# A recommendation tower on one core: the order of a few VectorE steps, look-ups and one load in the first tile's batches 0 to 2

## The chip, the cores and the metric

The kernel runs on one core of a Trainium2 chip. The metric is the device time of one execution in microseconds (us). The engines are named as in the profile: PE (TensorE) multiplies matrices, with its weight loads as PEld; DVE (VectorE), ACT (ScalarE) and POOL (GpSimd) are the others; SP and ACT also issue direct DMAs, POOL the gathers. Each engine works through its own list of instructions in order and waits at semaphores for the others.

## The reference, cut to what matters

```python
e = jnp.stack([tbl_0[ids[:, 0]], ..., tbl_38[ids[:, 38]]], axis=1)      # 2048 x 39 x 32
p = inputs[:, ROW, :]                # the 741 pairs i < j of the 39 fields
q = inputs[:, COL, :]
z = jnp.einsum('bpc,apc,bpa->bp', p, w, q)       # w: 32 x 741 x 32
h = jnp.concatenate([z, dense_ctx], axis=1)
h = jnp.maximum(h @ W_top1 + b_top1, 0.0)        # 757 -> 512
h = jnp.maximum(h @ W_top2 + b_top2, 0.0)        # 512 -> 256
y = h @ W_top3
```

Thirty-nine embedding tables are looked up, every pair of fields gives one number through its own 32x32 matrix, and three layers follow. The tables have 1,000 to 125,000 rows.

## The kernel before, in words

The 2048 rows are cut into 4 tiles of 512 (`NT`, `NB`). The 39 fields are cut into 10 chunks of up to four (`NG`, `C`); a chunk of a tile is written (t, g). The pairs are grouped into 200 units (`UNITS`): a unit is the product of one field j of chunk g with the four fields of chunk gi, so one 128-row matmul. Two units make a step, two steps a batch, and a tile has 50 batches (`NBAT`).

A batch b is, on PE: two steps of `interact` (L590, u_ps <- e4, w4: pair weights times the field stacked four times), then `reduce` of batch b-1 (L614, z_ps: sums over 32 rows), then what tables of numbers put there. A step waits until the products of two steps before are made. On DVE: `multiply` (L911), two products of 128x1024, prod <- u_ps, eT; then splits, one-hots and weights as the tables say.

A chunk comes in by one or both of two ways into one accumulator, `t_ps`. Fields in large tables are gathered by POOL (L419, `indirect_dma_start`), and turned on PE (`turn`, L534). Fields in small tables ("hot", `HOT_TABLES`: chunks 1, 2, 7, 8) are looked up: for each slice k, DVE makes a one-hot in bf16 (`one_hot_slice`, L899) and PE multiplies it by three bf16 parts of the table (`look_up`, L553). A slice holds up to four fields. Chunk 7 has ten slices: slices 0 to 7 have four fields (12 matmuls; on DVE one instruction of 125x1536 with `row8` and one of 125x512 with `row10`), slices 8 and 9 one field (3 matmuls, one instruction of 125x512). There are three one-hot buffers (`OS`): DVE waits at slice n for the look-up of slice n-3.

When `t_ps` is full, ACT takes it (`take_chunk`): parts <- t_ps (L717), the high part, and eT <- t_ps (L722). Only then may the next chunk use `t_ps`. DVE makes the low part (`split_chunk`, L865: eT minus the high part). In the first tile, chunks 1, 0, 2, 3, 7 (`MADE`) are stacked without memory: PE repeats the parts (`make_half`, L571, two fields of the chunk at a time, into m_ps and z_ps) and ACT copies them to e4 (`take_half`, L734 and L735). The second half waits for the copy of the first. All other chunks are stored by SP to memory (`scratch`) and come back stacked.

`FIRST_TILE` says for each chunk of tile 0 in which batch it is turned and in which batch each slice is looked up; from it come `TAKES` (batch to slices), `COMPLETE` (batch in which a chunk is complete) and the rest. DVE makes a batch's one-hots one batch ahead: after the products of batch b, it makes the slices of `TAKES[b+1]`. Chunk 2 is complete in batch 1; its first use is the second step of batch 2 (unit 10). Chunk 3 is first used in batch 5, chunk 7 in batch 9.

The pair weights are split too, in 13 pieces of 16 units (`PREP_UNITS`): ACT loads a piece (`load_weights`, L741), rounds it to the high part (L748) and stores that to `w_rows` (L751), DVE makes the low part (`weights_low`, L872), ACT stores it (L758). `PREPS` says in which batch a piece is made ({1: 2, 3: 3, 6: 4, ...}), `PREP_LOADS` in which it is loaded ({2: 3, 4: 4, 6: 5, ...}). Two rooms alternate, so piece 3's load waits only for piece 1's stores. SP brings finished pieces to PE as w4 (L436).

POOL's first 96 gathers are not paced by the products: gather n waits for the landing of gather n-3. In tile 0 the gathers 0 to 15 are chunk 0's, 16 to 19 chunk 2's, 20 to 35 chunk 3's, 36 to 51 chunk 4's, 52 to 67 chunk 5's. The turn of chunk 4 stands on PE in batch 7, after that batch's `reduce`. SP issues the five loads of the MLP's weights (L504) in batch 7.

Of the kernel before, what the change touches and what calls it, by code (L numbers as in the profile page):

```python
# [21 lines left out]
def fields_in(g):  # L22
    return min(C, F - C * g)
# [23 lines left out]
def slice_fields(g, k):  # L47

    return [x for x, n in enumerate(HOT_SLICES[g]) if n > k]
# [41 lines left out]
def place_sums():  # L91
# [4 lines left out]
    for g, gi, j in UNITS:  # L96
# [9 lines left out]
        if room > n:  # L106
# [24 lines left out]
PREP_UNITS = [(16 * k, min(NU, 16 * k + 16)) for k in range(-(-NU // 16))]  # L131
PREPS_FIRST = 2
PREPS = {max(4 * k - 11, 2 * k - 3 if k < 4 else 6): k for k in range(PREPS_FIRST, len(PREP_UNITS))}

PREP_LOADS = {max(2 if k == 3 else 4, 4 * k - 15, k + 1 if k > 4 else 0): k for k in range(3, len(PREP_UNITS))}

BEGIN = (1, 0)
FIRST_TILE = ((2, 0, 0, (0, 0, 0, 1, 1, 1, 1, 1)), (7, 0, None, (1, 1, 1, 1, 1, 2, 2, 2, 2, 2)), (3, 0, 3, ()), (4, 0, 7, ()),  # L140
# [9 lines left out]
MADE = ((0, 1), (0, 0), (0, 2), (0, 3), (0, 7))  # L150
# [8 lines left out]
def chunks_of_tile(t):  # L159
    return [x for x in (OTHER_TILES if t else FIRST_TILE) if t + x[1] < NT]  # L160

# [54 lines left out]
for t in range(NT):  # L216
    for g, nxt, turn, slices in chunks_of_tile(t):
        c = (t + nxt, g)
# [62 lines left out]
def tower(nc, tables, ids, hot_ids, hot_rows, dense, w, w1, b1, w2, b2, w3, sel_in, ident_in, y):  # L281
# [4 lines left out]
    with ExitStack() as ctx:  # L286
# [106 lines left out]
        def e_slot(t, g):  # L393
            return NG + TWO_PLACES.index(g) if t % 2 and g in TWO_PLACES else g
# [308 lines left out]
        def _(act):  # L703
# [33 lines left out]
            def load_weights(k):  # L737
                a, b = PREP_UNITS[k]
                if k >= 2:
                    act.wait_ge(s_wout[k % 2], 64 * (k // 2))  # L740
                act.dma_start(w_in_room[k % 2][:, 0:(b - a) * D], w[:, a * P:b * P].rearrange("a (s n) -> a s n", s=C)  # L741
                              ).then_inc(s_wraw[k % 2], 16)

            def weights_high(k):
                a, b = PREP_UNITS[k]
                n = (b - a) * D
                act.wait_ge(s_wraw[k % 2], 16 * (k // 2 + 1))
                nc.scalar.copy(w_hi_room[k % 2][:, 0:n], w_in_room[k % 2][:, 0:n]).then_inc(s_whi, 1)  # L748
                act.wait_ge(s_whi, k + 1)
                for h in range(2):  # L750
                    act.dma_start(w_rows[:, h, 0, a * P:b * P].rearrange("a (s n) -> a s n", s=C),  # L751
                                  w_hi_room[k % 2][:, 0:n].bitcast(F32)).then_inc(s_wout[k % 2], 16)
# [72 lines left out]
            for t in range(NT):  # L825
                for b in range(NBAT):
# [12 lines left out]
                    if t == 0:  # L839
# [8 lines left out]
                        if b in PREPS:  # L848
                            weights_high(PREPS[b])
                        if b in PREP_LOADS:  # L850
                            load_weights(PREP_LOADS[b])
            t = NT - 1
# [6 lines left out]
        def _(dve):  # L859
            def split_chunk(c):  # L860
                t, g = c
                n = POS[c]
                rows = D * fields_in(g)
                dve.wait_ge(s_et, n + 1)
                nc.vector.tensor_tensor(parts[0:rows, n % 2, 1, :], eT[0:rows, e_slot(t, g), :],  # L865
                                        parts[0:rows, n % 2, 0, :].bitcast(F32), ALU.subtract).then_inc(s_el, 1)

            def weights_low(k):
                a, b = PREP_UNITS[k]
                n = (b - a) * D  # L870
                dve.wait_ge(s_whi, k + 1)
                nc.vector.tensor_tensor(w_in_room[k % 2][:, 0:n].bitcast(F32R), w_in_room[k % 2][:, 0:n],  # L872
                                        w_hi_room[k % 2][:, 0:n].bitcast(F32), ALU.subtract).then_inc(s_wlo, 1)

            def table_rest(g):
                dve.wait_ge(s_thi, HOT_CHUNKS.index(g) + 1)
                nc.vector.tensor_tensor(table_room(g), table_room(g), table_part(g, 0), ALU.subtract).then_inc(s_tres, 1)

            def table_low(g):
                dve.wait_ge(s_tmid, HOT_CHUNKS.index(g) + 1)  # L880
                nc.vector.tensor_tensor(table_part(g, 2), table_room(g), table_part(g, 1), ALU.subtract).then_inc(s_tlo, 1)

            def one_hot_slice(c, k):
                t, g = c
                n = LOOK_BEFORE[c] + k
                if k == 0:
                    dve.wait_ge(s_hidx[LPOS[c] % 2], 16 * (LPOS[c] // 2 + 1))
                if n >= OS:
                    dve.wait_ge(s_look, n - OS + 1)
                fields = slice_fields(g, k)  # L890
                for tall in (False, True):
                    here = [(i, x) for i, x in enumerate(fields) if (HOT_SLICES[g][x] > HK) == tall]
                    for a, (i, x) in enumerate(here):
                        if a and here[a - 1][1] == x - 1:
                            continue
                        run = 1
                        while a + run < len(here) and here[a + run][1] == x + run:
                            run += 1
                        last = nc.vector.tensor_scalar(one_hot[0:HP, n % OS, i * NB:(i + run) * NB],  # L899
                                                       hot_idx[0:HP, LPOS[c] % 2, x * NB:(x + run) * NB],  # L900
                                                       (row10 if tall else row8)[0:HP, k:k + 1], None, ALU.is_equal)
                last.then_inc(s_hot, 1)

            def multiply(t, n):
                s = NS * t + n
                dve.wait_ge(s_u, s + 1)
                if s >= PR:
                    dve.wait_ge(s_red, s - PR + 1)
                a, b = sorted(e_slot(t, UNITS[UPS * n + i][1]) for i in range(UPS))
                e = eT[:, a:b + 1:b - a, :] if a != b else eT[:, a:a + 1, :].broadcast_to([P, UPS, NB])  # L910
                nc.vector.tensor_tensor(prod[:, s % PR, :, :], u_ps[:, s % 2, :, :], e, ALU.mult).then_inc(s_mul, 1)  # L911
# [29 lines left out]
            for t in range(NT):  # L941
                for b in range(NBAT):
                    for x in range(SPB):
                        multiply(t, SPB * b + x)
                    if t == 0 and b == 0:
                        table_low(7)
                    for c in COMPLETE.get(NBAT * t + b - 1, ()):
                        if c not in MADE:
                            split_chunk(c)
                    if t == 0:  # L950
                        if b == LAST_TABLE_BATCH + 1:
                            table_rest(HOT_CHUNKS[-1])
                        if b == LAST_TABLE_BATCH + 3:
                            table_low(HOT_CHUNKS[-1])
                        for c in COMPLETE.get(b, ()):
                            if c in MADE:
                                split_chunk(c)
                    for c, k in TAKES.get(NBAT * t + b + 1, ()):
                        one_hot_slice(c, k)
                    if t == 0 and b in PREPS:  # L960
                        weights_low(PREPS[b])

# [58 lines left out]
```

## Time and profile before

| | us |
|---|---|
| median of 3 runs | 761.44 |
| lowest, highest | 761.08, 764.19 |
| the profiled execution, its own time | 762.68 |
| its span, first to last instruction | 760.8 |

| engine | busy, us | share of the span |
|---|---|---|
| PE | 711.1 | 93% |
| DVE | 610.1 | 80% |
| POOL | 411.7 | 54% |
| ACT | 104.5 | 14% |

The profiled execution is 1.24 us above the median of the three runs. The page cuts the span in 40 slices of 19 us: PE is busy for 7 or 8 tenths of the slices in the first 150 us and 9 or more from there to the end. The first tile ends at about 200 us.

### The profile page before, as it was taken

Reading aid. Unit: us, or ns where it says so; the run is one execution under the profiler, and the core shown is the slowest. Engines: PE = TensorE matmul, PEld = TensorE weight load, DVE = VectorE, ACT = ScalarE, POOL = GpSimd, SP = SyncE. Lnnn points to the kernel's source line nnn. Section 1 sums busy time; section 2 is a strip of 40 time slices with the busy share of each in tenths; the row PEclk is TensorE's granted clock in tenths of the full one; section 3 lists DMA queues with packets and bytes.
Section 4 is the critical chain, followed back from the end, with each engine's and each line's share of the span. In section 5 each row is a group of like instructions: output and inputs, shape, how many; then the busy total and the mean of one; then the engine's idle time right before and its main releaser. Section 6 shows DMA issues by size and latency. Waiting matters only on the chain.

```text
span 760.8 us, 10920 instructions
## 1 busy us (share of the span) xinstructions
PE 711.1 (93%) x4202; PEld 285.7 (38%) x4202; DVE 610.1 (80%) x773; ACT 104.5 (14%) x186; POOL 411.7 (54%) x424
## 2 busy tenths in 40 slices
PE   0778888798999999999999999999999999999998
PEld 0233233333334444443434444444334434343343
DVE  3675798899989997998879987998879877788640
ACT  3413301111110100110110101011010101011002
POOL 5777546577776565667656555667655566000000
PEclk9787999999999999999999999999999999999999
DMA  7633987869868382739675472747656373553100
GB/s 205 192 115 87 321 314 235 312 217 307 288 212 289 112 264 75 243 72 307 179 243 184 143 259 64 234 117 243 226 185 233 100 253 88 167 174 105 69 0 0
DMA packets 72271, 141.40 MB, mean 186 GB/s; under 512 B 13829, under 2 KB 23704, under 8 KB 72092
## 3 DMA queue, kind: packets, MB, share of 16 engines
q1 hardware_dynamic: 48796, 116.86, 44.4%
q0 software_dynamic: 13440, 6.91, 6.6%
q10 hardware_dynamic: 9984, 16.94, 6.3%
q8 instruction: 33, 0.54, 0.3%
q14 instruction: 18, 0.15, 0.1%
HBM read 109.66 MB, written 31.00 MB: 185 GB/s over the span
## 4 chain that ended last, share of the span: by engine, by line
PE 81%; DVE 8%; issue 4%; DMA 3%; POOL 2%; ACT 1%; ACTq 0%; SPq 0%; DVEq 0%
PE z_ps L614 26%; PE u_ps L590 26%; PE t_ps L553 10%; PE m_ps L627 8%; DVE prod L911 5%; PE m_ps L629 3%; POOL e_rows L419 2%; DVE one_hot L899 2%; PE t_ps L534 2%; PE u_ps L649 1%; DMA e<-scratch 1%; PE u_ps L658 1%; PE m_ps L631 1%; PE t_ps L641 1%; PE m_ps L641 1%
## 5 line engine op out<-in xcount | busy, mean ns | idle before, releaser
L911 DVE TENSOR_TENSOR prod<-u_ps,eT 128x1024 f32<-128x1024 f32 x400 | 469.6, 1216 | 93.6 <-PE u_ps L590 92.7
L419 POOL DMA_INDIRECT e_rows<-in_tbl_dram,idx x420 | 411.5, 980 | 234.9 <-DVE prod L911 109.5
L590 PE MATMUL u_ps<-e,w 128*128 128x512 f32 x800 | 254.9, 433 | 17.8 <-DVE prod L911 12.9
L614 PE MATMUL z_ps<-prod,sel 128*32 128x512 f32 x1600 | 263.0, 613 | 0.0
L590 PEld LDWEIGHTS u_ps<-e,w 128*128 128x128 f32 x800 | 133.7, 190 | 159.8 <-DVE prod L911 75.8
L553 PE MATMUL t_ps<-one_hot,tb 125*32 125x512 bf16 x1344 | 134.1, 394 | 10.2 <-DVE one_hot L899 8.7
L899 DVE TENSOR_SCALAR one_hot<-hot_idx,row 125x512 bf16<-125x512 f16 (+2 forms) x296 | 108.2, 421 | 13.7 <-PE t_ps L553 11.9
L614 PEld LDWEIGHTS z_ps<-prod,sel 128*32 128x32 f32 x1600 | 43.6, 108 | 137.4 <-issue 111.1
L553 PEld LDWEIGHTS t_ps<-one_hot,tb 125*32 125x32 bf16 x1344 | 48.8, 98 | 91.5 <-issue 59.4
L627 PE MATMUL m_ps<-zT,w1s 128*128 128x512 f32 x144 | 73.5, 592 | 0.0
L717 ACT CAST parts<-t_ps 128x512 fp32r<-128x512 f32 (+1 forms) x40 | 23.5, 587 | 216.1 <-PE t_ps L553 125.1
L781 ACT COPY zT<-z_ps 128x512 f32<-128x512 f32 x24 | 14.1, 587 | 202.0 <-PE z_ps L614 202.0
L865 DVE TENSOR_TENSOR parts<-eT,parts 128x512 fp32r<-128x512 f32 (+1 forms) x40 | 27.2, 680 | 3.8 <-ACT eT L722 3.8
L627 PEld LDWEIGHTS m_ps<-zT,w1s 128*128 128x128 f32 x144 | 27.1, 188 | 6.3
L788 ACT ACTIVATE h<-m_ps,b1s 128x512 f32<-128x512 f32 x13 | 9.0, 689 | 138.4 <-PE m_ps L627 137.1
L629 PE MATMUL m_ps<-h,w2s 128*128 128x512 f32 x48 | 24.5, 592 | 0.0
L722 ACT COPY eT<-t_ps 128x512 f32<-128x512 f32 (+1 forms) x40 | 23.7, 591 | 0.0
L534 PEld LDWEIGHTS t_ps<-ident,e_rows 128*128 128x128 f32 (+2 forms) x112 | 12.2, 143 | 26.3 <-issue 22.9
L534 PE MATMUL t_ps<-ident,e_rows 128*128 128x128 f32 (+2 forms) x112 | 19.3, 298 | 2.6 <-DMA e_rows<-in_tbl_dram,idx 2.6
L872 DVE TENSOR_TENSOR h<-h 128x512 fp32r<-128x512 f32 (+1 forms) x13 | 8.6, 665 | 3.5 <-ACT h L748 3.5
L748 ACT CAST h<-h 128x512 fp32r<-128x512 f32 (+1 forms) x13 | 7.9, 608 | 19.0 <-DMA h<-in_w_dram 10.2
L629 PEld LDWEIGHTS m_ps<-h,w2s 128*128 128x128 f32 x48 | 9.0, 188 | 2.1
(52 smaller groups left out, 124.1 us busy)
## 6 DMA issues: line engine op xcount, KB each, us to landing
w<-w_rows SPq DMA_DIRECT2D x100, 512.0 KB
e<-scratch SPq DMA_DIRECT2D x62, 512.0 KB, 5.8
scratch<-parts SPq DMA_DIRECT2D x62, 256.0 KB
w_rows<-h ACTq DMA_DIRECT2D x48, 256.0 KB
e_rows<-in_tbl_dram,idx POOLq DMA_INDIRECT x420
hot_idx<-hot SPq DMA_DIRECT2D x12, 512.0 KB
h<-in_w_dram ACTq DMA_DIRECT2D x12, 256.0 KB, 4.8
e<-scratch SPq DMA_DIRECT2D x8, 384.0 KB
```

What stands on the lines that cost most here:

```text
L419: pool.indirect_dma_start(e_rows[:, r, n, D * q:D * q + D], None, tables[f], bass.IndirectOffsetOnAxis(ap=idx[:, t, f * TPG + n:f * TPG + ...
L534: last = nc.tensor.transpose(t_ps[0:hi, b * P:b * P + P], rows, ident[:, :])
L553: last = nc.tensor.matmul(t_ps[D * q:D * q + D, :], tb[0:HP, part, col:col + D], one_hot[0:HP, n % OS, here * NB:(here + 1) * NB], start=k ...
L590: last = nc.tensor.matmul(u_ps[:, s % 2, place, :], w4[:, p % WR, (u % PW) * P:(u % PW + 1) * P], e4[:, E4_SLOT[g], j - C * g, :], start=T ...
L614: last = nc.tensor.matmul(z_ps[D * quad:D * quad + D, z % 2, :], sel[:, D - 1 - row:2 * D - 1 - row], prod[:, (NS * t + n) % PR, place, :] ...
L627: last = nc.tensor.matmul(m_ps[:, :], w1s[:, k, m * P:m * P + P], zT[:, t % 2, k, :], start=k == 0, stop=stop)
L629: last = nc.tensor.matmul(m_ps[:, :], w2s[:, k, m * P:m * P + P], h1[:, k, :], start=k == 0, stop=stop)
L717: nc.scalar.copy(parts[0:rows, n % 2, 0, :], t_ps[0:rows, :]).then_inc(s_eh, 1)
L722: nc.scalar.copy(eT[0:rows, e_slot(t, g), :], t_ps[0:rows, :]).then_inc(s_et, 1)
L865: nc.vector.tensor_tensor(parts[0:rows, n % 2, 1, :], eT[0:rows, e_slot(t, g), :], parts[0:rows, n % 2, 0, :].bitcast(F32), ALU.subtract). ...
L899: last = nc.vector.tensor_scalar(one_hot[0:HP, n % OS, i * NB:(i + run) * NB], hot_idx[0:HP, LPOS[c] % 2, x * NB:(x + run) * NB], (row10 i ...
L911: nc.vector.tensor_tensor(prod[:, s % PR, :, :], u_ps[:, s % 2, :, :], e, ALU.mult).then_inc(s_mul, 1)
```

## The change

Three things change, all in the first tile.

1. DVE's split of chunk 2 (`split_chunk((0, 2))`) stood behind the products of batch 1; now it stands behind the one-hots that precede those products.
2. Chunk 7's slices 3 and 4 go from batch 1 to batch 2, on PE (`look_up`) and on DVE (`one_hot_slice`). Batch 1 then has five slices of chunk 2 and three of chunk 7, batch 2 has seven of chunk 7.
3. ACT issues the load of piece 3 of the pair weights (the fourth) in batch 1 instead of batch 2.

```diff
-PREP_LOADS = {max(2 if k == 3 else 4, 4 * k - 15, k + 1 if k > 4 else 0): k for k in range(3, len(PREP_UNITS))}
+PREP_LOADS = {max(1 if k == 3 else 4, 4 * k - 15, k + 1 if k > 4 else 0): k for k in range(3, len(PREP_UNITS))}
...
-FIRST_TILE = ((2, 0, 0, (0, 0, 0, 1, 1, 1, 1, 1)), (7, 0, None, (1, 1, 1, 1, 1, 2, 2, 2, 2, 2)), (3, 0, 3, ()), (4, 0, 7, ()),
+FIRST_TILE = ((2, 0, 0, (0, 0, 0, 1, 1, 1, 1, 1)), (7, 0, None, (1, 1, 1, 2, 2, 2, 2, 2, 2, 2)), (3, 0, 3, ()), (4, 0, 7, ()),
...
                         for c in COMPLETE.get(b, ()):
-                            if c in MADE:
+                            if c in MADE and c != (0, 2):
                                 split_chunk(c)
                     for c, k in TAKES.get(NBAT * t + b + 1, ()):
                         one_hot_slice(c, k)
+                    if t == 0 and b == 0:
+                        split_chunk((0, 2))
```

On DVE, at the end of batch 0 and the start of batch 1 (`prod` is a batch's products, `parts` the split of chunk 2, each pair of `one_hot` rows with row8 and row10 one slice of chunk 7; - is before, + the change, and the same happens to slice 3's pair, just ahead of these rows):

```order
-L899 TENSOR_SCALAR one_hot<-hot_idx,row8 125x1536
-L899 TENSOR_SCALAR one_hot<-hot_idx,row10 125x512
-L911 TENSOR_TENSOR prod<-u_ps,eT 128x1024 x2
-L865 TENSOR_TENSOR parts<-eT,parts 128x512
+L865 TENSOR_TENSOR parts<-eT,parts 128x512
+L911 TENSOR_TENSOR prod<-u_ps,eT 128x1024 x2
+L899 TENSOR_SCALAR one_hot<-hot_idx,row8 125x1536
+L899 TENSOR_SCALAR one_hot<-hot_idx,row10 125x512
```

The split went ahead of the products, and slices 3 and 4 went behind both.

On PE, batch 1 (first piece) and batch 2 (second piece); t_ps rows are look-ups, the m_ps and z_ps rows with `parts` are `make_half` of chunk 2:

```order
 L590 MATMUL u_ps<-e4,w4 128x512 x4
 L614 MATMUL z_ps<-prod,sel 32x512 x4
-L553 MATMUL t_ps<-one_hot,tb 32x512 x105
+L553 MATMUL t_ps<-one_hot,tb 32x512 x81
 L571 MATMUL m_ps<-parts,rep 128x512 x2
 L571 MATMUL z_ps<-parts,rep 128x512 x2
```

```order
 L590 MATMUL u_ps<-e4,w4 128x512 x4
 L614 MATMUL z_ps<-prod,sel 32x512 x4
-L553 MATMUL t_ps<-one_hot,tb 32x512 x42
+L553 MATMUL t_ps<-one_hot,tb 32x512 x66
 L590 MATMUL u_ps<-e4,w4 128x512 x4
 L614 MATMUL z_ps<-prod,sel 32x512 x4
```

Twenty-four matmuls, two slices, moved from ahead of `make_half` of chunk 2 to the end of batch 2.

On ACT, batches 1 and 2 (L748 and L751 are piece 2's high part and its stores, L741 the load of piece 3, L717 and L722 the taking of chunk 7, L758 the stores of piece 2's low part):

```order
 L748 CAST h1<-h1 128x512
 L751 DMA w_rows<-h1 32x4x512 x2
+L741 DMA h1<-in_w_dram 128x1x512
 L717 CAST parts<-t_ps 128x512
 L722 COPY eT<-t_ps 128x512
 L772 CAST tb<-zT 125x1216
 L758 DMA w_rows<-h1 32x4x512 x2
-L741 DMA h1<-in_w_dram 128x1x512
```

The load no longer stands behind the taking of chunk 7. POOL and SP have the same order before and after.

## Rows read from the trace of the kernel before

**Rows 1.** The page: busy tenths and granted clock, span in 40 slices.
```profile
PE   0778888798999999999999999999999999999998
...
PEclk9787999999999999999999999999999999999999
```

**Rows 2.** Stretches: busy us of PE, PEld, DVE, ACT, POOL; granted clock; DMA share; GB/s.
```profile
43.74:57.38 13.64, 10.29 (x134) 4.32 (x130) 10.54 (x20) 1.07 (x2) 10.37 (x11) 1.00 0.28 84
57.39:67.62 10.23, 8.76 (x41) 2.81 (x41) 2.19 (x6) 2.67 (x5) 7.79 (x9) 0.50 0.22 64
67.63:81.27 13.64, 10.49 (x68) 4.27 (x64) 11.23 (x13) 6.49 (x11) 8.66 (x9) 1.00 0.62 190
81.28:84.69 3.41, 3.41 (x11) 0.71 (x9) 3.30 (x3) 0.62 (x1) 1.39 (x2) 0.50 1.04 404
...
122.24:125.65 3.41, 3.41 (x12) 1.00 (x12) 2.61 (x3) 0.62 (x1) 2.78 (x3) 0.50 0.98 310
...
135.89:139.30 3.41, 3.35 (x12) 1.07 (x13) 2.12 (x4) 0.00 (x0) 1.60 (x2) 0.50 0.95 317
```

**Rows 3.** PE in order of time, 50 to 64: start, us, work [idle before <- releaser].
```profile
51.43 3.67 PE L553 MATMUL t_ps<-one_hot,tb 125*32 125x512 bf16 x60 [1.23 <-ACT eT L722]
57.22 0.61 PE L571 MATMUL m_ps<-parts,rep 32*128 32x512 f32 x1 [2.12 <-DVE parts L865]
...
59.63 0.76 PE L571 MATMUL m_ps<-parts,rep 32*128 32x512 f32 x1 [1.31 <-ACT e L735]
...
62.16 1.19 PE L590 MATMUL u_ps<-e,w 128*128 128x512 f32 x2 [0.16 <-ACT e L735]
63.29 1.92 PE L614 MATMUL z_ps<-prod,sel 128*32 128x512 f32 x5
```

**Rows 4.** PE in order of time, short windows: slices 0 to 2, then 5.
```profile
51.43 2.13 PE L553 MATMUL t_ps<-one_hot,tb 125*32 125x512 bf16 x36 [1.23 <-ACT eT L722]
...
66.71 1.27 PE L553 MATMUL t_ps<-one_hot,tb 125*32 125x512 bf16 x12
```

**Rows 5.** DVE in order of time, 47 to 83.
```profile
48.00 3.68 DVE L899 TENSOR_SCALAR one_hot<-hot_idx,row 125x1536 bf16<-125x1536 f16 x8 [2.46 <-PE t_ps L553]
52.32 1.90 DVE L899 TENSOR_SCALAR one_hot<-hot_idx,row 125x1536 bf16<-125x1536 f16 x4 [0.64 <-PE t_ps L553]
54.13 2.34 DVE L911 TENSOR_TENSOR prod<-u_ps,eT 128x1024 f32<-128x1024 f32 x2
56.40 0.67 DVE L865 TENSOR_TENSOR parts<-eT,parts 128x512 fp32r<-128x512 f32 x1
57.00 2.59 DVE L899 TENSOR_SCALAR one_hot<-hot_idx,row 125x1536 bf16<-125x1536 f16 x6
68.04 0.35 DVE L899 TENSOR_SCALAR one_hot<-hot_idx,row 125x512 bf16<-125x512 f16 x1 [8.46 <-PE t_ps L553]
68.69 0.35 DVE L899 TENSOR_SCALAR one_hot<-hot_idx,row 125x512 bf16<-125x512 f16 x1 [0.29 <-PE t_ps L553]
68.96 0.68 DVE L872 TENSOR_TENSOR h<-h 128x512 fp32r<-128x512 f32 x1
69.56 2.35 DVE L911 TENSOR_TENSOR prod<-u_ps,eT 128x1024 f32<-128x1024 f32 x2
...
77.23 2.35 DVE L911 TENSOR_TENSOR prod<-u_ps,eT 128x1024 f32<-128x1024 f32 x2
81.39 2.35 DVE L911 TENSOR_TENSOR prod<-u_ps,eT 128x1024 f32<-128x1024 f32 x2 [1.82 <-PE u_ps L590]
```

**Rows 6.** ACT in order of time: chunk 2 taken, piece 3's load, its rounding.
```profile
50.79 0.59 ACT L722 COPY eT<-t_ps 128x512 f32<-128x512 f32 x1
...
72.04 0.63 ACTq L741 DMA_DIRECT2D h<-in_w_dram  x1
...
75.61 0.62 ACT L748 CAST h<-h 128x512 fp32r<-128x512 f32 x1 [0.17 <-DMA h<-in_w_dram]
```

**Rows 7.** PE in order of time: chunk 3's halves, first and second, next step.
```profile
76.81 0.46 PE L571 MATMUL m_ps<-parts,rep 32*128 32x512 f32 x1 [0.26 <-issue]
...
78.89 0.46 PE L571 MATMUL m_ps<-parts,rep 32*128 32x512 f32 x1 [1.35 <-ACT e L735]
...
80.85 1.31 PE L590 MATMUL u_ps<-e,w 128*128 128x512 f32 x3 [0.79 <-ACT e L735]
```

**Rows 8.** PE in order of time, short windows: batch 0's reduce at full clock.
```profile
45.90 0.64 PE L614 MATMUL z_ps<-prod,sel 128*32 128x512 f32 x3
...
47.21 0.59 PE L614 MATMUL z_ps<-prod,sel 128*32 128x512 f32 x1
47.23 0.83 PE L553 MATMUL t_ps<-one_hot,tb 125*32 125x512 bf16 x9
```

**Rows 9.** POOL in order of time: gathers 48, 54, 59 and 62, counted from 0.
```profile
70.99 0.95 POOL L419 DMA_INDIRECT e_rows<-in_tbl_dram,idx  x1 [0.30 <-issue]
...
82.99 0.94 POOL L419 DMA_INDIRECT e_rows<-in_tbl_dram,idx  x1 [3.43 <-DMA e_rows<-in_tbl_dram,idx]
...
92.61 0.94 POOL L419 DMA_INDIRECT e_rows<-in_tbl_dram,idx  x1 [2.97 <-DMA e_rows<-in_tbl_dram,idx]
...
99.05 0.94 POOL L419 DMA_INDIRECT e_rows<-in_tbl_dram,idx  x1 [3.00 <-DMA e_rows<-in_tbl_dram,idx]
```

**Rows 10.** PE in order of time: the turn of chunk 4 and the next step.
```profile
90.77 0.66 PE L534 MATMUL t_ps<-ident,e_rows 128*128 128x128 f32 x4
92.31 0.73 PE L590 MATMUL u_ps<-e,w 128*128 128x512 f32 x2 [0.88 <-DVE prod L911]
```

## The prediction, made before the changed kernel ran

> **What bounds the kernel now.** I read the page's 40 slices first [rows 1]: from about 150 us to the end PE is busy for nine tenths or more, so whatever reaches that part later or earlier shifts the end with it. Before that PE has holes, and the change is in these holes. Next the stretches cut where the granted clock changes [rows 2]: 57.39 to 67.62 is the longest stretch at 0.50 (1.2 GHz) after 44 us; PE is busy in it for 8.76 of 10.23 us, but at half speed. Then the engines in order of time. On PE [rows 3] chunk 2's first half starts at 57.22 after 2.12 us of idling, released by DVE's split; the second half waits 1.31 us for ACT's copy, and the step that needs chunk 2 starts at 62.16. On DVE [rows 5] the split at 56.40 stands behind two pairs of one-hots that waited for look-ups (52.32, 1.90 us) and behind two products (54.13, 2.34 us). But eT and the high part were there at 50.79 + 0.59 = 51.38 [rows 6]. So the split ran 5.0 us after its inputs were ready, and PE stood still for it. After that DVE in turn waits 8.46 us, until 68.04, for a look-up [rows 5]: PE is the bound from 57.2 to 68, DVE from there to 79.6 (one block of work, first wait 1.82 us at 81.39).
>
> **The change part by part.** I follow the point at which batch 2's products start on DVE: 69.56 before.
>
> Split and slices 3 and 4 (one edit in effect). DVE's one-hots up to slice 2 of chunk 7 end at 48.00 + 3.68 = 51.68 [rows 5]. The split (0.67 us) finds its input ready and ends at 52.3, in the place where DVE now idles 0.64 us. The products follow until 54.6, earlier than before. PE looks up slices 0 to 2 from 51.43 for 2.13 us [rows 4], to 53.5. The split is done, so the first half starts at 53.5 instead of 57.22: **-3.7 us**, of which 1.4 is the work that moved away (2 slices of 2.13 / 3 = 0.71) and the rest the wait of 2.12 and what DVE held up in slices 3 and 4.
>
> The two halves. Before, at 0.50, it was 4.94 us from the first half (57.22) to the step that needs the second (62.16) [rows 3]. Chunk 3's halves at the full clock took 76.81 to 80.85 = 4.04 us [rows 7]. The clock is still full at 53.5 [rows 2], so the step starts at 57.5: another **-0.9**.
>
> Step and reduce. Here the clock has to be chosen. PE is idle for about 1.35 + 0.8 us in those 4 us [rows 7], and right after that pattern the clock fell at 81.28 [rows 2]; I take it that it falls at about 57.4 here too. After 57.5 PE has unbroken work, as it had after 80.85, and there the low stretch lasted 3.41 us, as in the other two short ones [rows 2]; before, the halves' gaps lay inside it and it lasted 10.23. So I take 57.4 to 60.8 at low clock. The step then takes 62.16 to 63.29 = 1.13 us as before, to 58.65. The reduce took 63.29 to 66.71 = 3.42 us at low clock [rows 3, 4]; at full clock three of its four rounds take 45.90 to 47.21 = 1.31 [rows 8], so 1.75 in all. 2.15 us of it at low clock do 63%, the rest takes 0.65: first look-up at 61.45 instead of 66.71, another **-0.65**, in all -5.25.
>
> Seven slices instead of five. Slice 3, 4 and 5 have their one-hots (three pairs at 2.59 / 3 = 0.87 us from 54.6 [rows 5]). For slice 6 DVE waits, because of the three buffers, for slice 3's look-up, which ends at 61.45 + 0.7 = 62.15. Then one-hots 6 and 7 until 63.95, slice 8 (0.35) until 64.3, slice 9 after look-up 6 (64.3) until 64.6, the weights' low part (68.96 to 69.56 = 0.6) and the products at 65.15 to 65.2. From the first look-up that is 3.75 us where it was 69.56 - 66.71 = 2.85: **+0.9**. DVE and PE meet there: slices 7, 8 and 9 end on PE at about 66.3 and the first product at 66.4, so neither holds the next step up by itself.
>
> Sum: -3.7 - 0.9 - 0.65 + 0.9 = **-4.35**, products at 65.2 instead of 69.56. With the reduce and the first slices wholly at low clock (first look-up at 62.1, slices of 1.27 us [rows 4] until 64.2) it is 66.7, -2.85. With no low stretch (step 0.73 [rows 10], reduce 1.75) it is 63.7, -5.9.
>
> The clock, row first: it was low from 57.39 to 67.62 and came back within the look-ups [rows 2]. The Trainium skill (TensorE: Matmul & The Clock Gate, Part 1: The HAM clock gate) says that the throttled state is the default, activity releases it, and how many matmuls run cold differs from run to run. By that rule the length I chose is one of several for the same program, and the sum moves between the two ends above.
>
> Piece 3's load. It took 72.04 to 75.6, and ACT waited 0.17 us for it [rows 6]. DVE had other work until 77.23 in any case [rows 5], so at the old place it cost nothing; if everything moves by 4.35 it would move too. Early, its 256 KB go at about 60 us, in a stretch whose DMA share is 0.22 [rows 2]. I take **0** (ends: -0.17, and 0 the other way, since its room is free and piece 2's stores stand ahead of it).
>
> What comes after. DVE's block from 69.56 to 79.6 starts earlier as a whole, with the DMAs that ACT and SP issue behind it. POOL's gathers do not: they are paced by their own landings. Chunk 4's turn stands at 90.77 [rows 10] and would come at 86.4. Its last gather, 51, had landed when 54 was issued at 82.99 [rows 9]; by then three gathers fewer are through when the crowded stretch begins, so it fares like gather 54 before, which had landed when 57 was issued at 87.45, so by 87.45 - 4.35 = 83.1 at the latest. 3.3 us are left, so I carry all of -4.35 to the end. The profiled execution then takes 762.68 - 4.35 = 758.3; against the median of the runs, 761.44, 757.1. I forecast **757.1 us**.
>
> **The rivals.**
>
> A. More clock comes back. Three more low stretches of 3.41 us follow idle spells at 77 to 81, 119 to 121 and 134 to 136 [rows 2]. Half speed costs up to 1.7 us in each. With other spacing one of them may fail to come, or that at 57.4 may not: 757.1 - 1.6 = 755.5. For it: the spell at 77 to 81 is made of two short gaps. Against it: the same work with the same gaps stands there after the change.
>
> B. The low clock holds until about 64: -2.85, 758.6. For it: from 60.8 to 63.3 PE was nearly always busy and the clock stayed low [rows 2, 3]. Against it: that stretch began with gaps.
>
> C. The low stretch keeps its 10 us. Then slices 3 to 7 take 1.27 each from 62.1, to 68.4, slices 8 and 9 (half speed of 0.65) end at 71.0, and PE's next step, at 70.8 before (69.56 and one product), comes at 71.0: the two moved slices take back everything, 761.6.
>
> D. Slower: the gathers. If gather 51 falls behind the MLP's five loads, which SP would issue at about 82.0 (on PE's progress), it lands as 56 or as 59 did. Those let 59 and 62 go at 92.61 and 99.05 [rows 9], so 88.3 or 94.7 with the shift. The turn at 94.7 is 3.9 us later than before; 0.88 us of that is slack in front of the next step [rows 10]: +3.0, 764.4. It decides from a landing after 90.8 on. Against it: one whole gather of margin, and 3.3 us. The row shows that a gather issued behind these loads took some 5 us. The Trainium skill (DMA: Bandwidth & Descriptors, Queues, rings and completion order) says that each DMA engine takes turns between its queues, packet by packet; by that rule a few rows of a gather would not be held so long, and D would vanish.
>
> That the change does not do what it says can be left out: the order of the instructions on DVE and PE shows both moves, and the split's input at 51.38 precedes its new place at 51.68.
>
> **How the numbers follow.** Forecast (755.9 to 758.2, with the clock as chosen) 0.47; A 0.16; B 0.23; C 0.08; D 0.06. What a measurement of this kernel can tell from no change is about 0.5%, 3.8 us: faster means below 757.6. Of the forecast's 0.47 about 0.34 lies below, A wholly, B hardly (0.02): faster 0.52. D's 0.06 goes to slower only in part (above 765.2); with other late gathers or a further low stretch I give slower 0.04. The same takes the rest, 0.44. The range leaves out D, most of C and the far part of A: 754.6 to 760.6.
>
> **What would show it.** In the profile of the changed kernel: DVE's split at 51.6 to 52.3 with no wait; PE's first half of chunk 2 at 53.5, the second at 55.6, the step at 57.5; a low stretch of 3.4 us there; the first look-up of batch 2 at 61.4; DVE's one short wait at 57 to 62 for slice 3's look-up; batch 2's products at 65.2; then chunk 3's halves at 72.5 and the turn of chunk 4 at 86.4 with no wait for a gather. Wrong would be: a low stretch that lasts beyond 64 (B, C), PE idle before the turn of chunk 4 (D), or a wait of PE for e or w that was not there before and gives the gain back between 86 and 150.

## The result, and the profile after

| | before | changed |
|---|---|---|
| median, 20 runs each, us | 762.0 | 759.6 |
| lowest, highest | 760.77, 764.19 | 757.48, 763.0 |
| ratio (95% interval) | | 0.9969 (0.9959 to 0.9979) |
| span of the profiled execution | 760.8 | 758.8 |

The change makes the kernel 0.31% faster, -2.4 us. The forecast was 757.1 us, a gain of 4.35 us, and a gain clear of 0.5% was held the likelier case. The sign and the range (754.6 to 760.6) were right, the size was almost double of what came.

PE, then DVE, then ACT of the changed kernel in order of time (start, us, work, idle before it and releaser); they answer to [rows 3, 5, 6]:

```profile
50.56 2.13 PE L553 MATMUL t_ps<-one_hot,tb 125*32 125x512 bf16 x36 [1.23 <-ACT eT L722]
52.62 0.49 PE L571 MATMUL m_ps<-parts,rep 32*128 32x512 f32 x1
...
54.66 0.47 PE L571 MATMUL m_ps<-parts,rep 32*128 32x512 f32 x1 [1.31 <-ACT e L735]
...
56.70 1.19 PE L590 MATMUL u_ps<-e,w 128*128 128x512 f32 x2 [0.64 <-ACT e L735]
57.83 1.92 PE L614 MATMUL z_ps<-prod,sel 128*32 128x512 f32 x5
```
```profile
61.25 1.49 PE L553 MATMUL t_ps<-one_hot,tb 125*32 125x512 bf16 x12
```
```profile
50.71 0.68 DVE L865 TENSOR_TENSOR parts<-eT,parts 128x512 fp32r<-128x512 f32 x1
51.31 2.34 DVE L911 TENSOR_TENSOR prod<-u_ps,eT 128x1024 f32<-128x1024 f32 x2
...
62.80 2.43 DVE L899 TENSOR_SCALAR one_hot<-hot_idx,row 125x1536 bf16<-125x1536 f16 x6 [6.77 <-PE t_ps L553]
65.14 0.68 DVE L872 TENSOR_TENSOR h<-h 128x512 fp32r<-128x512 f32 x1
65.75 2.35 DVE L911 TENSOR_TENSOR prod<-u_ps,eT 128x1024 f32<-128x1024 f32 x2
```
```profile
58.33 0.62 ACTq L741 DMA_DIRECT2D h<-in_w_dram  x1
...
71.52 0.63 ACT L748 CAST h<-h 128x512 fp32r<-128x512 f32 x1
```

DVE's split (50.71) now runs as soon as its input is there, and PE starts the first half (52.62) right behind look-up 2 with no idle time. All of this execution is 0.87 us early (chunk 7's first look-up at 50.56, before at 51.43), so from here on I count from that look-up. The two profiles then give:

| us from chunk 7's first look-up | before | forecast | changed |
|---|---|---|---|
| first half of chunk 2 | 5.79 | 2.07 | 2.06 |
| step that needs chunk 2 | 10.73 | 6.07 | 6.14 |
| first look-up of batch 2 | 15.28 | 10.02 | 10.69 |
| batch 2's products | 18.13 | 13.78 | 15.19 |

The stretches of the changed kernel by granted clock (busy us of PE, PEld, DVE, ACT, POOL; clock; DMA share; GB/s), beside [rows 2]:

```profile
42.41:56.04 13.63, 11.09 (x125) 4.80 (x118) 11.53 (x21) 2.70 (x6) 10.25 (x9) 1.00 0.32 97
56.06:62.87 6.81, 6.17 (x35) 1.81 (x36) 0.07 (x1) 1.02 (x3) 5.16 (x6) 0.50 0.43 129
62.88:76.52 13.64, 11.02 (x82) 4.51 (x77) 12.74 (x17) 5.49 (x10) 10.28 (x9) 1.00 0.48 149
76.54:83.34 6.80, 6.34 (x16) 1.95 (x16) 3.70 (x3) 1.51 (x2) 3.34 (x4) 0.50 0.87 321
```

The clock was low (0.50) for 6.8 us, not for 3.4, and again 6.8 us at chunk 3's halves, where before had 3.41. So the first two rows of the table came as worked out. The third is 0.67 us late and the fourth 1.41, and both lie in or behind the low stretch: my first theory was that the clock took the missing part. It needed runs, since two executions are two draws.

### The profile page after: what moved, and what is told of

It is laid out like the page before. It is cut to its first block, busy times and chain, and to the rows that moved or that the text cites. A ratio compares the mean times of both kernels' runs of the same rounds, so it can differ in the third digit from the quotient of the medians.

```text
span 758.8 us, 10920 instructions
## 1 busy us (share of the span) xinstructions
PE 709.1 (93%) x4202; PEld 285.5 (38%) x4202; DVE 610.1 (80%) x773; ACT 104.3 (14%) x186; POOL 414.7 (55%) x424
## 4 chain that ended last, share of the span: by engine, by line
PE 81%; DVE 8%; issue 4%; DMA 3%; POOL 2%; ACT 1%; SPq 0%; ACTq 0%; DVEq 0%
PE z_ps L614 26%; PE u_ps L590 26%; PE t_ps L553 10%; PE m_ps L627 8%; DVE prod L911 5%; PE m_ps L629 3%; POOL e_rows L419 2%; PE t_ps L534 2%; DVE one_hot L899 2%; DMA e<-scratch 1%; PE u_ps L649 1%; PE u_ps L658 1%; PE m_ps L631 1%; PE t_ps L641 1%; PE m_ps L641 1%
## 5 line engine op out<-in xcount | busy, mean ns | idle before, releaser
L553 PE MATMUL t_ps<-one_hot,tb 125*32 125x512 bf16 x1344 | 133.6, 392 | 10.8 <-DVE one_hot L899 9.4
L717 ACT CAST parts<-t_ps 128x512 fp32r<-128x512 f32 (+1 forms) x40 | 23.5, 587 | 217.5 <-PE t_ps L553 126.4
L722 ACT COPY eT<-t_ps 128x512 f32<-128x512 f32 (+1 forms) x40 | 23.7, 591 | 0.0
L748 ACT CAST h<-h 128x512 fp32r<-128x512 f32 (+1 forms) x13 | 7.9, 609 | 16.2 <-issue 9.1
```

The costliest lines, as they stand in the source:

```text
L553: last = nc.tensor.matmul(t_ps[D * q:D * q + D, :], tb[0:HP, part, col:col + D], one_hot[0:HP, n % OS, here * NB:(here + 1) * NB], start=k ...
L717: nc.scalar.copy(parts[0:rows, n % 2, 0, :], t_ps[0:rows, :]).then_inc(s_eh, 1)
L722: nc.scalar.copy(eT[0:rows, e_slot(t, g), :], t_ps[0:rows, :]).then_inc(s_et, 1)
```

## The experiments

Times are medians in us, given beside the runs of the kernel before on the same chip, then the ratio with its 95% interval in brackets. "To the products" is always from chunk 7's first look-up to batch 2's products, read off each kernel's rows.

**The first four** fell on a chip where the kernel before itself took 887.65 us.

> The changed kernel once more, for a second profile beside the runs of its parts. My theory after the result: the mechanism of the prediction holds (first half of chunk 2 about 3.8 us sooner, seen from the moment chunk 7's look-ups begin), and the low stretch of the clock, whose length differs from run to run, takes part of the gain. It expects the ratio to before at 0.997 again (about -2.3 us), the first half right behind look-up 2 with no wait, and a low stretch of another start or length than in the first profile. The rival, that the clock is a fixed thing of the program and the first profile (products of batch 2 at 65.75) is what always happens, expects the same stretches within 0.5 us.

> Before, with DVE's split of chunk 2 ahead of the products alone (slices 3 and 4 stay in batch 1). Slices 3 and 4 keep PE busy until 55.1 and DVE until 54.2, so the split ends at 54.8 and the first half starts at about 55.2 instead of 57.2: -2.0 us at the halves, and batch 2 keeps its five slices, so none of it is paid back there. Theory that the split carries the gain: -1.5 to -2.5 us in the time, 760.0 where before has 762.0. Rival, that the slices carry it: within 0.7 us of before.

```diff
-                            if c in MADE:
+                            if c in MADE and c != (0, 2):
...
+                    if t == 0 and b == 0:
+                        split_chunk((0, 2))
```

> Before, with slices 3 and 4 in batch 2 alone (split stays behind the products). One-hots end at 51.7, products at 54.0, split at 54.7, first half at 54.8 instead of 57.2: -2.4 us; two more slices in batch 2 cost 0.9 to 1.4 us, more at low clock. Theory: -0.5 to -1.5 us in the time. Rival, that the slices carry the gain: -2 us or more.

```diff
-(7, 0, None, (1, 1, 1, 1, 1, 2, 2, 2, 2, 2))
+(7, 0, None, (1, 1, 1, 2, 2, 2, 2, 2, 2, 2))
```

> The changed kernel with the load of piece 3 back in batch 2. Theory: the load was worth nothing, so the same time as the changed kernel within 0.5 us, ACT waiting under 0.3 us for it in front of its rounding. Rival: with the earlier look-ups the load lands too late and holds ACT and DVE by 1 us or more, time nearer to before.

```diff
-PREP_LOADS = {max(1 if k == 3 else 4, ...
+PREP_LOADS = {max(2 if k == 3 else 4, ...
```

They took 879.9, 885.5, 888.0 and 883.8 us. In x1's profile the DMA share is 0.08 and the granted clock 0.50 from 30 to 60 us:

```profile
30.00:60.00 30.00, 6.03 (x28) 0.93 (x22) 2.05 (x6) 0.00 (x0) 22.69 (x25) 0.50 0.08 13
```

Chunk 7's look-ups began at 128 to 131 us there. What held that chip was not looked into. None of the theories of these four can be judged by them; all four kernels were run again on other chips (v1, y4, v3, v4).

**The clock taken out.** Matmuls that nobody reads go into PE's gaps.

> The changed kernel with matmuls whose results nobody reads in the gaps that the halves of chunks 2 and 3 leave on PE (4 between the halves, 2 in front of the step that needs them), so that PE has no idle spell there. Theory, that the clock takes the missing part of the gain: no low stretch between chunk 7's first look-up and chunk 4's turn; from that first look-up to batch 2's products 12.3 us, where the first profile of the changed kernel has 15.19 and before 18.13; time 3 to 4 us under the changed kernel, so about -5.5 to -6 us to before (756.2 where before has 762.0). Rival, that the missing part lies in DVE's waits for its three buffers and in PE's own work: at most 1 us off the changed kernel.

> The kernel before with the same fillers, and 6 more ahead of chunk 2's first half, where PE idles 2.12 us. Theory: no low stretch there either; first look-up of chunk 7 to batch 2's products 14.5 us instead of 18.13, time 3 to 5 us under before (758). The difference to the changed kernel with fillers is then what the change is worth at a steady clock: 2.2 us. Rival: within 1 us of before.

```diff
+            def filler(n, to_u, to_t=0):
...
+                for i in range(n):
+                    to = t_ps[:, :] if to_t else u_ps[:, to_u % 2, i % 2, :]
+                    nc.tensor.matmul(to, w4[:, piece, 0:P], e4[:, E4_SLOT[1], 0, :], start=True, stop=True)
...
+                            if (c, half) == ((0, 2), 0) and PRE:
+                                filler(PRE, 4)
                             make_half(c, half)
+                            if (c, half) == ((0, 2), 0) and MID:
+                                filler(MID, 4)
+                            if c == (0, 3) and MID3:
+                                filler((MID3, 2)[half], 0, 1)
...
+                        if (t, b, x) == (0, 2, 1) and STEP5:
+                            filler(STEP5, 5)
                         interact(t, SPB * b + x)
```

Neither had a low stretch between the first look-up and the products. DVE's rows of the products, the changed kernel with fillers (its first look-up at 51.03) and before with fillers (51.79):

```profile
63.26 2.35 DVE L932 TENSOR_TENSOR prod<-u_ps,eT 128x1024 f32<-128x1024 f32 x2
```
```profile
66.21 2.35 DVE L932 TENSOR_TENSOR prod<-u_ps,eT 128x1024 f32<-128x1024 f32 x2
```

To the products: 12.23 and 14.42, as expected (12.3 and 14.5). **At a steady clock the change is worth 2.2 us there.** But the times were 759.54 and 759.60 beside 761.49, ratios 0.9974 (0.9955 to 0.9993) and 0.9978 (0.9959 to 0.9997): no better than the change alone, where I had expected -5.5 to -6 and -3 to -5. Something gives the time back further on. PE's turns, first of the changed kernel with fillers, then of before with fillers:

```profile
91.36 1.11 PE L535 MATMUL t_ps<-ident,e_rows 128*128 128x128 f32 x4 [8.49 <-DMA e_rows<-in_tbl_dram,idx]
```
```profile
228.00 0.63 PE L535 MATMUL t_ps<-ident,e_rows 128*128 128x128 f32 x4 [2.96 <-DMA e_rows<-in_tbl_dram,idx]
```

The first is chunk 4's turn, which waits 8.49 us for its gathers: rival D of the prediction, at a larger gain than the change has. It is not the usual case: this profiled execution took 763.77 us, the most of the twelve. Chunk 4's last gather, 51, went out 10.8 us later in it than before. The stream was late ahead of the fillers too: gather 30 at 49.90, before at 47.61. Gather 51, first with fillers, then before:

```profile
86.25 0.94 POOL L420 DMA_INDIRECT e_rows<-in_tbl_dram,idx  x1 [2.96 <-DMA e_rows<-in_tbl_dram,idx]
```
```profile
75.43 1.50 POOL L419 DMA_INDIRECT e_rows<-in_tbl_dram,idx  x1 [0.30 <-issue]
```

The other waiting turn is that of chunk (1, 3) in the second tile, whose last gather is 143. It stood at 230.97 before.

**Real work in the gaps**, and the split alone once more.

> The changed kernel with real work in the gaps instead of fillers: PE does the first step of batch 2 between chunk 2's halves and the reduce of batch 1 ahead of the second step. Theory: the work fills about 0.7 of 1.35 us in the first gap and all of the second, so the clock mostly stays up, and 1.75 us of reduce no longer stand behind the copy: 2 to 3 us under the changed kernel, 757 where before has 762.0. Rival: reduce now waits for DVE's products of batch 1 and nothing is won.

```diff
                             make_half(c, half)
+                            if (c, half) == ((0, 2), 0):
+                                interact(0, 4)
...
+                        if (t, b, x) == (0, 2, 0):
+                            reduce(0, 1)
+                            continue
                         interact(t, SPB * b + x)
...
                     if b:
-                        reduce(t, b - 1)
+                        if (t, b) != (0, 2):
+                            reduce(t, b - 1)
```

To the products it took 11.03 us, the shortest with three gathers in flight, with no low stretch on the way. The time was 759.85 beside 761.49, 0.998 (0.9963 to 0.9996): again nothing beyond the change. Its turns of chunk 4 and (1, 3) both wait:

```profile
85.83 0.66 PE L534 MATMUL t_ps<-ident,e_rows 128*128 128x128 f32 x4 [2.27 <-DMA e_rows<-in_tbl_dram,idx]
```
```profile
227.69 0.95 PE L534 MATMUL t_ps<-ident,e_rows 128*128 128x128 f32 x4 [3.71 <-DMA e_rows<-in_tbl_dram,idx]
```

> Split alone once more, on another chip than the first time, where all kernels took 880 us. Theory, from the first run's stretches (first look-up of chunk 7 to batch 2's products 15.27 us there, against 17.03 for the whole change): -2 us or more to before, as good as the whole change or better, because slices 3 and 4 keep PE busy between look-up and halves and do not come back behind them. Rival: the slices carry the gain, and this is within 0.7 us of before.

759.73 beside 761.49, 0.9988 (0.9972 to 1.0005). The median is -1.8 us, but the interval takes in no change, so the times alone decide for neither theory. In its profile the first half stood 3.61 us after the first look-up and the products 14.26, with one low stretch of 3.4.

**The gathers let loose.**

> The kernel before with four unpaced gathers in flight instead of three (gather n waits for the landing of n-4), nothing else. Control for the next three. In its profile no turn waits for a gather, so both theories expect no change to speak of: within 1 us of before, the last gather of the first tile's successor chunk (1, 3), number 143, landing some us sooner than at 222.2.

```diff
-WINDOW = 3
+WINDOW = 4
```

> The kernel before with fillers in PE's gaps and four gathers in flight. With three in flight the fillers put the products of step 60 6.35 us sooner (counted from chunk 7's first look-up), but PE then waited 2.96 us at the turn of chunk (1, 3) for gather 143, and the end was 2.4 us sooner. Theory, that this turn is the point that gives the gain back: no wait there now, 143 landing at 222 or before, and time 5 to 6 us under before (756). Rival, that something else in the second tile pulls the time back: again about -2 us.

> The changed kernel with four gathers in flight. Theory: in some of its executions the turn of chunk (1, 3), 231.0 before and 229.0 in the changed kernel's first profile with gather 143 at 225.6, comes against the gather; with four in flight it never does, so the spread of its times shrinks at no cost and the median falls by 0.5 to 1.5 us: 758 to 759 where the change alone gave 759.6. Rival: the clock alone takes the missing part of the gain, no difference to the changed kernel.

> The changed kernel with real work in the gaps (a step between the halves of chunk 2, the reduce ahead of the next step) and four gathers in flight. With three in flight its products of step 60 were 6.8 us sooner than before, the end 2.2. Theory: the end is now 5 to 6.5 us sooner, 755 to 756.5, the best so far. Rival: about 759.5 as with three.

| kernel | with three | with four gathers in flight |
|---|---|---|
| before | (the kernel itself) | 1.0 (0.9985 to 1.0014) |
| before, fillers | 0.9978 (0.9959 to 0.9997) | 0.9938 (0.9919 to 0.9958) |
| changed | 0.9969 (0.9959 to 0.9979) | 0.9967 (0.995 to 0.9983) |
| changed, real work in the gaps | 0.998 (0.9963 to 0.9996) | 0.9927 (0.9908 to 0.9945) |

The control, before with four, shows no change (its medians, 761.35 beside 762.39, lie near the lower edge of the interval). So the gathers are what cut the larger gains: the fillers' time falls to 757.74 and the reordered kernel's to **756.16 us beside 762.39**, better than both kernels of this case. The changed kernel with fillers was not run with four. PE's turn of chunk (1, 3) in the reordered kernel comes with no wait:

```profile
221.94 0.66 PE L534 MATMUL t_ps<-ident,e_rows 128*128 128x128 f32 x4
```

The line that was changed (`WINDOW`) governs only the first 96 gathers, and 143 is not one of them. The rows of POOL show how it reaches 143: with three in flight gather 95 went out at 159.74 (v1, below), with four at 141.39 (z4). From there to 143 POOL in v1 issued one gather in 1.3 us, with no idle time but 0.30 us between two of them. What the first 96 lose is therefore still missing at 143, which went out at 223.25 and at 209.43.

For the changed kernel itself four gathers in flight bring nothing that can be measured, as the rival said, and the spread did not shrink either (756.67 to 763.14 over 12 runs).

**More draws of the clock.**

> The changed kernel, a further profile on a chip that is not slowed down. What the runs with fillers left: at a steady clock the change is worth 2.2 us (14.41 against 12.23 from chunk 7's first look-up to batch 2's products). Theory: the prediction's other 2.2 us were clock, and the changed kernel gets them in some executions only. It expects products of batch 2 at 13.6 us (one low stretch of 3.41 since the first look-up), 15.2 (two) or about 17 (three) from the first look-up, not a fixed value, and a mean granted clock over the runs no higher than before's by more than 0.001. Rival: the first profile (15.19) is the rule and half the gain is always lost in the same place.

760.06 beside 762.17, 0.9964 (0.9945 to 0.9983). Its stretches:

```profile
43.58:57.21 13.63, 10.50 (x118) 4.50 (x109) 10.38 (x20) 3.29 (x7) 9.93 (x10) 1.00 0.24 72
57.23:60.62 3.39, 3.33 (x15) 1.06 (x16) 0.00 (x0) 0.43 (x1) 2.53 (x3) 0.50 0.48 164
60.64:74.28 13.64, 11.35 (x101) 4.46 (x94) 12.16 (x17) 4.85 (x8) 9.67 (x11) 1.00 0.49 139
74.30:81.10 6.80, 6.31 (x16) 2.06 (x16) 4.30 (x4) 2.18 (x3) 3.38 (x4) 0.50 0.99 373
```

Here the low stretch is the 3.4 us of the forecast, and DVE's products start at 64.93, 13.80 after the first look-up (51.13); the forecast was 13.78. Yet the span was 758.9, as in the first profile. Part of the gain went at chunk 3's halves, with 6.8 us of low clock, and part at the turn of (1, 3):

```profile
229.08 0.63 PE L534 MATMUL t_ps<-ident,e_rows 128*128 128x128 f32 x4 [1.91 <-DMA e_rows<-in_tbl_dram,idx]
```

One part of the expectation missed: the mean granted clock of the ten runs was 0.9814 and that of before's 33 on this chip 0.9794, so 0.0020 more and not at most 0.001.

> The kernel before as an experiment of its own, for a second profile. Theory: from chunk 7's first look-up to batch 2's products 17.8 to 18.1 us with a low stretch of 10.24 us, as in the two profiles so far that have the old order (with three and with four gathers in flight): its gaps lie so that the long low stretch comes each time, while the changed kernel's varies. Rival: before varies as much, 16.5 to 18.1.

761.66 beside 762.17, 0.9993 (0.9978 to 1.0007). This is the kernel before against itself, and no difference is right. The theory falls, the rival holds: before varies as well. Its low stretch was 6.8 us and the products stood at 66.58, 16.43 after its first look-up (50.15), not 18:

```profile
56.61:63.42 6.81, 5.50 (x19) 2.09 (x22) 1.47 (x4) 2.60 (x5) 5.20 (x6) 0.50 0.25 73
```

> Slices 3 and 4 in batch 2 alone, again, since the first time fell on a chip where all kernels took 880 us. Products of batch 1 end at 54.0, split at 54.7, first half 3.2 us after chunk 7's first look-up plus about 0.9: 4.0 after it (3.96 on the slow chip), where before has 5.6 to 5.8, the split alone 3.61 and both together 2.06. Theory: -0.5 to -1.5 us in the time, less than the split alone (-1 to -1.8). Rival: as much as both together.

761.59 beside 762.17, 0.9988 (0.9972 to 1.0003): -0.6 us, within the noise. That fits the lower end of the theory and no gain at all. The first half stood at 3.35 and the products at 16.39, with 6.8 us of low clock.

> The changed kernel without the earlier load of piece 3, again for the same reason. Theory: within 0.7 us of the changed kernel, ACT waiting under 0.5 us for the load in front of its rounding (L748). Rival: with everything else earlier the load at its old place holds ACT and DVE by 1 us or more.

760.74 beside 762.17, 0.9973 (0.9958 to 0.9988), against 0.9964 and 0.9969 of the whole change. ACT waited 0.43 us for the load. A small gain of the load, up to 0.7 us, is neither shown nor excluded. In this profile the turn of (1, 3) waited 2.62 us, and that of chunk 4 waited too:

```profile
89.09 0.66 PE L534 MATMUL t_ps<-ident,e_rows 128*128 128x128 f32 x4 [0.99 <-DMA e_rows<-in_tbl_dram,idx]
```

> The changed kernel with four gathers in flight once more. Its first 12 runs had a median of 759.86, no better than the change alone, though its profile had a span of 755.1, and the last profile of the change alone lost about 2 us between the products of step 60 and step 99, where the turn of chunk (1, 3) met gather 143. Theory, that the gathers cut the changed kernel too in many executions: 757.5 to 759, about 1 us under the changed kernel (760.0). Rival, that they cut only larger gains than this one: 759.5 to 760.5.

759.93 beside 761.36, 0.9979 (0.9966 to 0.9992). The rival again: over the 30 runs of the changed kernel and the 24 with four gathers in flight the medians are 759.74 and 759.86.

> The kernel before with DVE's split early, slices 3 and 4 of chunk 7 left in batch 1, the load left in batch 2, the step and the reduce in the halves' gaps, and four gathers in flight. It tells what slices 3 and 4 are worth once the gaps are filled. They keep PE busy until 3.6 us after chunk 7's first look-up, then halves, step and reduce, then five slices instead of seven: products of batch 2 at 11 to 11.5 us after the first look-up, as with the slices moved (11.13). Theory: 756 to 757, the same as the moved slices within 0.8 us. Rival, that moving them is worth its 1.2 us here too: 757.5.

756.48 beside 761.36, 0.9933 (0.9913 to 0.9952); to the products 11.05 us, with slices moved 11.13. Once the gaps are filled, moving slices 3 and 4 is worth nothing that can be measured: 0.9933 here and 0.9927 with them moved (z4, another chip, six runs each).

The parts at equal lengths of the low stretch, us to the products:

| low stretch | before | slices alone | split alone | whole change |
|---|---|---|---|---|
| 6.8 us | 16.43 | 16.39 | | 15.19 |
| 3.4 us | | | 14.26 | 13.80 |

At the products the split carries the gain. The slices alone give nothing, and beside the split some 0.5 us. That is one profile each; the whole change with one other edit (no early load, four gathers) lies within 0.2 us of it: 15.18 and 15.29 at 6.8, 13.64 at 3.4. The times of the parts are too close to each other to say the same.

## Why the prediction was wrong, by its own steps

Two steps failed. The sum rests on one low stretch of 3.41 us after the change, where the first profile had 6.8 (step and reduce, seven slices), subtracted from a base with 10.24 us of it, which is as variable; and the gain at batch 2's products was carried whole to the end, where less than half of it arrived in the profiles.

**What bounds the kernel:** right. The split ran late, PE stood for it, and DVE afterwards waited for look-ups.

**Split and slices, -3.7:** right; 5.79 to 2.06 is -3.73.

**The two halves, -0.9:** right in this profile (4.08 us from half to step, 4.04 expected), since the clock was still full.

**Step and reduce, -0.65:** this term failed. It took one low stretch of 3.4 us as given because PE had unbroken work. The profiles of kernels with the changed order show 6.8, 3.4, 3.4 (four gathers in flight), 6.8 (four) and 6.8 (without the load) us of it before the products. In the first, the reduce was wholly at low clock, 57.83 to 61.25 = 3.42, and the term came to nothing.

**Seven slices, +0.9:** +1.65 there (61.25 to 65.75 is 4.50, before 2.85), because slice 3 ran at low clock too. With one stretch of 3.4 the whole sum was hit to 0.02 us (v1): the working was right, and the length of the stretch was a guess that held in two of five profiles.

**"I carry all of it to the end":** this step failed too, and without it a gain of 4.35 at the products would still not be one at the end.

| us from chunk 7's first look-up | before | before again (v2) | changed | changed again (v1) |
|---|---|---|---|---|
| batch 2's products | 18.13 | 16.43 | 15.19 | 13.80 |
| turn of chunk 4 | 39.34 | 38.77 | 37.65 | 35.90 |
| turn of chunk (1, 3) | 179.54 | 179.23 | 178.43 | 177.95 |
| end of the span | 709.4 | 709.1 | 708.2 | 707.8 |

In v1 the sum came true, 4.33 us at the products, and 1.6 of it reached the end: 0.9 went by the turn of chunk 4, where the low stretch at chunk 3's halves lasted 6.8 us instead of 3.41, and 1.85 by the turn of (1, 3), which waited 1.91 us. In the first profile 1.2 of 2.94 reached the end, though no turn waited: 1.25 went by the turn of chunk 4, with 6.8 us of low clock at chunk 3's halves again, and 0.6 by the turn of (1, 3). Between the two one step waited 2.9 us for its stacked chunk from memory, where before it was 2.2. Chunk 4's turn waited for no gather in either, as said (88.21 and 87.03), but it did wait 0.99 us in the kernel without the load. And I looked at one turn only: that of (1, 3), 140 us later, is closer. How much each of the two costs the median is open; four gathers in flight did not make the changed kernel faster, so the waits at the turns can hardly be the larger part of it.

**The base was a draw too.** I subtracted from a profile with 10.24 us of low clock between first look-up and products. The second profile of before had 6.8 and was 1.7 us shorter there, of which 0.3 was left at the end. Of the 4.35, 2.2 were the change (the pair with fillers) and the rest the difference of two stretches, each of which varies.

The runs' own mean clocks point the same way. One stretch of 3.41 us at half speed lowers the mean over 760 us by 0.0022 (half of 3.41, divided by 760). All 91 runs of before that ran beside the y, z and v runs have a mean clock of 0.9800, the 30 runs of the changed kernel 0.9808. Among runs with 0.980 the mean times are 761.99 (41 runs) and 759.88 (12), with 0.982 760.64 (18) and 759.14 (12). At equal clock the change gives -1.5 to -2.1, near the 2.2 of the fillers; the clock adds about half a microsecond and not the two that the sum had from it. These figures mix chips. On v1's chip alone the clocks were 0.0020 apart, so there its share may be more than twice as large.

**Rivals.** B (the clock stays low until 64, products at 66.7) is what the first profile shows: 62.88 and 65.75, or 63.75 and 66.62 on the old count. B's time of 758.6 was still 1 us under the median. C did not occur. D did not occur in the changed kernel, and came true in one execution with fillers, at its place, with 8.49 us; there the gathers were late before chunk 7's look-ups began, not only behind the MLP's five loads. By the Trainium skill's rule that each DMA engine takes turns between its queues (DMA: Bandwidth & Descriptors, Queues, rings and completion order) the prediction had D vanish. In that execution it did not: the turn came 5.1 us after gather 51 had gone out (86.25 to 91.36). A's bonus did not come in the first profile, where three later low stretches came as before and the first of them was longer. It did come in one profile with four gathers in flight (z3), with none at chunk 3's halves and 756.95 us, while the median of that kernel stayed at 759.86.

**Piece 3's load, 0:** not contradicted.

## What to carry to other kernels

A term of a sum that rests on the granted clock in one profile is a draw, on both sides of the subtraction; size the edit at one clock level and give the clock a range of its own. Where one engine's work runs by its own pace (here the gathers) it puts a floor under every later meeting point: list the slack at all of them, and expect it to move by microseconds from execution to execution (gather 51 went out at 75.43 and 79.61 in the two profiles of before, at 80.08 and 79.15 in those of the changed kernel). A gain at one meeting point is not yet a gain at the end: read the later ones too. Here it paid best to fill the gaps between dependent small steps with work that was due soon anyway: that kept the clock up and took the work off the path (to the products 11.03 us, against 12.23 with fillers).

## What the runs showed of the hardware

The same program had its first low stretch after 55 us last 10.2 us in one execution and 6.8 in the other; the changed one 6.8 and 3.4. At chunk 2's halves with their two gaps of 1.3 and 0.6 us the clock fell in every profile of the changed kernel outside the first four runs; with matmuls in the gaps, useful or not, it stayed up until batch 2's products in all six. At chunk 3's halves, with their gaps left open, it fell for 3.4 or 6.8 us in every profile outside the first four runs but z3's. The Trainium skill (TensorE: Matmul & The Clock Gate, Part 1: The HAM clock gate) says, of the start of a kernel, that the number of matmuls at the low clock differs from run to run; the traces show the same 50 us into this one, with 3.4 to 10.2 us at one place.
